# Pads in front of each bucket, a tile table laid over partitions, and row numbers kept aside in a routed two-layer graph and expert kernel

## What is computed

```python
x = x + gnn(layernorm(x), adj)      # two layers: scores h h^T, softmax, mask adj, three projections
x = x + ffn(layernorm(x))           # routed experts, below
# ffn, with 8 experts of width 64, on the 16384 tokens xt:
route_prob = softmax((xt @ enc_w + enc_b) @ sw_w + sw_b)
routes     = argmax(route_prob)                       # one expert e for each token
out        = (gelu(xt @ w1[e] + b1[e]) @ w2[e] + b2[e]) * max(route_prob)
```

## Time and profile before

| | |
|---|---|
| time, median of 3 executions (lowest, highest) | 2221.36 us (2217.87, 2224.03) |
| profiled execution | 2229.13 us |
| its span, first to last instruction | 2227.4 us |
| mean granted TensorE clock, share of full speed | 0.986 |
| PE, DVE, ACT, POOL busy, share of the span | 95%, 75%, 67%, 63% |
| graph stage | from 0 to about 1938 us of the span |
| hand-over, last count to first tile's normalise | 1938 to 1956 us |
| expert stage | 1956 to 2227 us |

### The profile page before, as it was taken

How to read it: one execution, slowest core, us unless ns; L and a number is a source line. 1 busy time by engine, 2 the same in 40 slices (tenths; PEclk the granted TensorE clock), 3 DMA queues, 4 the chain that set the end, 5 groups by cost and what they waited for, 6 DMA issues and landing times. The chain is left out here.

```text
span 2227.4 us, 56587 instructions
## 1 busy us (share of the span) xinstructions
PE 2116.7 (95%) x13576; PEld 2035.7 (91%) x13577; DVE 1661.4 (75%) x5442; ACT 1496.4 (67%) x3901; POOL 1405.0 (63%) x3274
## 2 busy tenths in 40 slices
PE   6999999999999999999999999999999999578886
PEld 5999999999999999999999998999999999456665
DVE  4777777777777777777777776777777777657775
ACT  4777777677676776677777766776777766356664
POOL 2556666666666666666666666666666666535555
PEclk9999999999999999999999999999999999789998
DMA  7101111111111111111111111111111111256664
GB/s 188 31 26 49 49 37 49 49 45 49 41 45 49 49 45 50 42 49 49 49 43 47 49 49 42 45 49 49 46 48 41 45 49 33 105 184 208 221 224 144
DMA packets 94261, 153.77 MB, mean 69 GB/s; under 512 B 17627, under 2 KB 70700, under 8 KB 93954
## 3 DMA queue, kind: packets, MB, share of 16 engines
q1 hardware_dynamic: 75844, 99.61, 15.1%
q0 software_dynamic: 17408, 50.62, 6.0%
q10 hardware_dynamic: 704, 0.10, 0.0%
HBM read 96.11 MB, written 57.32 MB: 69 GB/s over the span
## 5 line engine op out<-in xcount | busy, mean ns | idle before, releaser
L421 PE MATMUL bank<-wT_hi,hT_hi 128*128 128x384 f32 x2304 | 797.9, 346 | 11.4 <-issue 5.4
L423 PE MATMUL bank<-wT_hi,hT_lo 128*128 128x384 f32 x2304 | 774.5, 336 | 0.0
L422 PE MATMUL bank<-wT_lo,hT_hi 128*128 128x384 f32 x2304 | 773.0, 336 | 0.0
L421 PEld LDWEIGHTS bank<-wT_hi,hT_hi 128*128 128x128 f32 x2304 | 434.9, 189 | 19.2 <-ACT bank L614 11.1
L422 PEld LDWEIGHTS bank<-wT_lo,hT_hi 128*128 128x128 f32 x2304 | 435.0, 189 | 0.0
L423 PEld LDWEIGHTS bank<-wT_hi,hT_lo 128*128 128x128 f32 x2304 | 433.8, 188 | 0.0
L1145 POOL TENSOR_TENSOR hT_lo<-hT,hT_hi 128x384 fp32r<-128x384 f32 x256 | 263.5, 1029 | 23.9 <-ACT hT_hi L679 22.4
L674 ACT ACTIVATE hT<-bank 128x384 f32<-128x384 f32 x256 | 126.1, 493 | 202.5 <-PE bank L413 180.9
L650 ACT CAST right_hi<-bank 128x384 fp32r<-128x384 f32 x256 | 123.0, 480 | 180.1 <-PE bank L423 179.2
L1548 POOL DMA_INDIRECT out_dram<-out_rows,tok x144 | 144.1, 1000 | 136.4 <-DVE out_rows L1519 100.7
L1200 POOL TENSOR_SCALAR_AFFINE_SELECT deltaT_hi<-turned_hi 128x128 fp32r<-128x128 f32 x256 | 87.7, 343 | 216.0 <-ACT turned_hi L656 208.5
(11 more groups left out here) (183 smaller groups left out, 5142.9 us busy)
## 6 DMA issues: line engine op xcount, KB each, us to landing
tok<-buckets SPq DMA_DIRECT2D x72, 388.0 KB
x_in<-in_x_dram SPq DMA_DIRECT2D x128, 192.0 KB, 2.5
x_res<-in_x_dram SPq DMA_DIRECT2D x128, 192.0 KB, 2.4
adj_in<-in_adj_dram SPq DMA_DIRECT2D x128, 64.0 KB, 2.4
buckets<-pads SPq DMA_DIRECT2D x9, 388.0 KB
out_dram<-out_rows,tok POOLq DMA_INDIRECT x144
buckets<-rows,dest_words POOLq DMA_INDIRECT x128, 2.8
w_top<-in_L_ffn_w_dram SPq DMA_DIRECT2D x2, 768.0 KB
```

The costliest lines, as they stand in the source:

```text
L421: pe.matmul(o, hi, w_hi, start=False, stop=False, skip_group_check=True)
L422: pe.matmul(o, hi, w_lo, start=False, stop=False, skip_group_check=True)
L423: last = pe.matmul(o, lo, w_hi, start=False, stop=(c == C - 1), skip_group_check=True)
```

## The change

1. **Pads in front.** A bucket's rows now begin FRONT = 256 rows behind its start, and the pads stand in those first 256 rows. Their nine stores need no computed row any more; SP issues them in the graph stage, behind the three loads of step 26 (PAD_STEP). An expert's last tile no longer runs on into pads behind the bucket: it begins 256 rows before the bucket's end, and so holds again some rows of the tile before it (or pads, for an expert with one tile).
2. **Tile table over partitions.** `tile_table` has tile number n on partition n, with operands of 72x8 or 72x64 and a few 72x1; its results lie in a column and are turned into rows by PE. A further result, `again`, gives for each row of each tile a large number where the row is one that the tile before has had, so that it is not written twice.
3. **Row numbers aside.** In step j+2 POOL adds the `ID` words of `tok[k]` and `again` into `row_ids[k]` (semaphore `ids_kept`), and the stores take their row numbers from there. SP's load of tile j waits for the combine of tile j-8 and for `ids_kept` in place of `stored`.

```diff
@@ graph stage, SP
                     def first_steps(i, key):
                         step(i, key)
+                        if isinstance(i, int) and i == PAD_STEP:
+                            sp.wait_ge(pads_made, 1)
+                            for row in [e * CAP for e in range(E)] + [TAIL]:
+                                sp.dma_start(buckets[row:row + TILE, :]..., pads[:]).then_inc(pads_stored, 16)
...
                     steps(sp, first_steps)
-                    sp.wait_ge(pads_made, 1)
-                    sp.dma_start(buckets[TAIL:TAIL + TILE, :]..., pads[:]).then_inc(pads_stored, 16)
-                    sp.wait_ge(ends_ready, 1)
-                    for e in range(E):
-                        row = sp.value_load(end_words[0:1, e:e + 1], min_val=e * CAP, max_val=e * CAP + TOKENS)
-                        sp.dma_start(buckets[bass.ds(row, TILE), :]..., pads[:]).then_inc(pads_stored, 16)
@@ PE, behind the last count
+                    pe.wait_ge(table_done, 2)
+                    pe.transpose(rows_of, per_tile["row"][0:TILES, :], ident[0:TILES, 0:TILES])
+                    pe.transpose(experts_of, per_tile["expert_at_most"][0:TILES, :], ident[0:TILES, 0:TILES]
+                                 ).then_inc(table_turned, 1)
+                    pe.wait_ge(table_done, 3)
+                    pe.matmul(twice_of, per_tile["twice_wide"][0:TILES, :], ident[0:TILES, 0:TILES], ...
+                              ).then_inc(table_turned, 1)
@@ DVE, tile_table: the dependent steps now, each one small operation
   held -> rough -> rounded -> tiles_of -> lower_tiles -> tiles_upto -> behind -> expert -> own_end -> end
        -> in_buckets -> row -> (PE turns) -> tile_row, tile_expert -> twice_wide -> (PE turns) -> again (x2)
@@ POOL, setup: iotas of 1x512, 1x576, 1x8, 1x64 give way to six, each of 128 partitions and at most 64 elements
@@ expert stage, SP load
                         if past(j, RING):
-                            sp.wait_ge(stored[k % OUT_RING], 16 * T // OUT_RING * (j - RING - k % OUT_RING) + 16 * T)
+                            sp.wait_ge(y_ready, T * (j - RING) + T)
+                            sp.nop(nofuse=True)
+                            sp.wait_ge(ids_kept, j - RING + 1)
@@ expert stage, POOL
+                    def keep_ids(j, k):
+                        pool.wait_ge(tok_loaded[k], 16 // RING * (j - k) + 16)
+                        if past(j, RING):
+                            pool.wait_ge(stored[k % OUT_RING], 16 * T // OUT_RING * (j - RING - k % OUT_RING) + 16 * T)
+                        pool.nop(nofuse=True)
+                        pool.tensor_tensor(row_ids[k][:], tok[k][:, :, ID].bitcast(I32),
+                                           again[:, j, :] ..., ALU.add).then_inc(ids_kept, 1)
+
                     def store(j, k):
+                        pool.wait_ge(ids_kept, j + 1)
                         for t in range(T):
...
-                                bass.IndirectOffsetOnAxis(ap=tok[k][:, t, ID:ID + 1].bitcast(U32), axis=0),
+                                bass.IndirectOffsetOnAxis(ap=row_ids[k][:, t:t + 1].bitcast(U32), axis=0),
...
                     def step(i, k):
+                        if there(i - 2):
+                            keep_ids(i - 2, (k - 2) % RING)
                         if there(i - DEPTH):
                             store(i - DEPTH, (k - DEPTH) % RING)
```

More of the change, by code:

```diff
@@ L157, in build @@
             w2_spare_bottom = ring_sb(2, "w2_spare_bottom", [P, D], F32R)
[L159 to L166, removed]
+            per_tile = {}
+            for name, shape in (("bases", [P, E]), ("held", [P, E]), ("rough", [P, E]), ("rounded", [P, E]),
+                                ("tiles_of", [P, E]), ("lower", [P, E, E]), ("lower_tiles", [P, E, E]),
+                                ("tiles_upto", [P, E]), ("behind", [P, E]), ("skipped", [P, E]), ("skip", [P, 1]),
+                                ("expert", [P, 1]), ("expert_at_most", [P, 1]), ("experts", [P, E + 1]),
+                                ("ends", [P, E + 1]), ("own_end", [P, E + 1]), ("end", [P, 1]), ("number", [P, 1]),
+                                ("straight", [P, 1]), ("twice", [P, 1]), ("twice_wide", [P, P]), ("position", [P, T]), ("in_expert", [P, 1]), ("in_buckets", [P, 1]), ("row", [P, 1])):
+                per_tile[name] = sb(f"per_tile_{name}", shape, F32, gnn_ctx)
             x_loaded = [sem(f"x_loaded{k}") for k in range(2)]
@@ L1005, in tile_table @@
[L1005 to L1012, removed]
@@ L1013, in tile_table @@
[L1013 to L1015 removed]
+                        dve.wait_ge(table, 8)
+                        dve.tensor_reduce(o["expert"], o["behind"], AX_X, ALU.add).then_inc(table, 1)
+                        dve.tensor_tensor_reduce(o["skipped"], o["behind"], o["tiles_of"], 1.0, 0.0, ALU.mult, ALU.add,
+                                                 o["skip"]).then_inc(table, 1)
@@ L1016, in tile_table @@
                         dve.wait_ge(table, 11)
-                        dve.scalar_tensor_tensor(o["row"][:], o["numbers"][:, :, 0], float(TILE), o["rows_before"][:],
+                        dve.tensor_reduce(o["end"], o["own_end"], AX_X, ALU.add).then_inc(table, 1)
+                        dve.wait_ge(table, 12)
+                        dve.scalar_tensor_tensor(o["in_buckets"], o["expert"], float(CAP), o["in_expert"],
                                                  ALU.mult, ALU.add).then_inc(table, 1)
-                        dve.wait_ge(table, 12)
@@ L1020, in tile_table @@
-                        dve.tensor_scalar(tile_row[:], o["row"][:], float(TAIL), None, ALU.min).then_inc(tiles_ready, 1)
+                        dve.wait_ge(table, 14)
+                        dve.tensor_scalar(o["row"], o["end"], -float(TILE), o["in_buckets"][:, 0:1], ALU.add, ALU.min
+                                          ).then_inc(table_done, 1)
+                        dve.wait_ge(table_done, 2)
+                        dve.tensor_tensor(o["twice"], o["in_buckets"], o["row"], ALU.subtract).then_inc(table, 1)
@@ L1022, in constants @@
+                        for t in range(T):
+                            dve.tensor_scalar(again[:, :, t], twice_of, per_tile["position"][:, t:t + 1], float(2 * TOKENS),
+                                              ALU.is_gt, ALU.mult).then_inc(tiles_ready, 1)
                     def constants():
```

94 lines of the change are left out of this document (60 added, 34 removed).

## The result

The changed kernel takes 2162.1 us (median of 4 runs, 2160.5 to 2163.8) against 2221.7 us for the kernel before, run beside it: a ratio of 0.973 (95% interval 0.972 to 0.9745), 59.6 us less. I had forecast 2180 with a range of 2166 to 2206: the direction was right, and the time lies under the range.

What follows compares the result with a forecast made beforehand. The prediction took a ring over the store's landing, 3.53 us a tile, to bound the expert stage. Loop -36.8, drain +1 and hand-over -5.7 gave -41.5 us, from a median of 2221.36 to 2180 us, range 2166 to 2206.

Steps and rivals of the forecast that it cites:

- stops of 10.5 us: Expert loop: ACT's unnamed waits and a lower clock, estimated at 10.5 us, would remain after the change.
- the price of `keep_ids` on POOL: Expert loop: the added POOL operation costs 0.25 us a tile, between 0.17 and 0.53.
- A ring over the store's landing: Expert loop: combine, store, landing, load and normalise must fit into three steps, 10.6 us, setting 3.53 us a tile.
- POOL's pace: Expert loop after the change: POOL's two stores and `keep_ids` need 2.83 us, so the pace is 2.85 us a tile.
- The base: Old expert loop: 63 steps between first and last normalise take 226.9 us, from which the loop's gain was counted.
- PE's floor: Expert loop: PE needs 2.66 us a tile, read from the first tiles, whose tokens are there in advance.
- my rival with 0.15: Expert loop: PE sets the pace, 2.66 to 2.75 us a tile, `keep_ids` hiding between stores; 2168 us, chance 0.15.
- The first eight tiles: Start of the expert loop: these tiles don't change, 0 us.
- Hand-over: Graph to expert stage: without pad stores the first load goes out near 1947.2, -5.7 us (-4.6 to -7.6).
- Pads in the graph stage: Step 26 of the graph stage: nine pad stores fit into 13.5 us on SP and cost nothing, at worst some 5 us.
- The constants: Setup: the shorter iotas are off the path, 0 us.
- The drain: Behind the last normalise: POOL's stores are already back to back, and the few `keep_ids` there cost +1 us.

Runs made afterwards that it cites:

- before_fourth: The kernel before, unchanged, profiled in another execution with increments on time: 2220.5 us.
- wait_stored: The changed kernel with the load of tile j waiting again for the store of tile j-8 to land: 2216.1 us, ratio 0.997.
- ids_only: The kernel before with part 3 of the change alone (row numbers copied aside, load waits for the combine): 2171.1 us, ratio 0.977.
- after: The changed kernel itself, as first profiled: an execution of 2160.5 us, median 2162.1 us.
- ids_by_dve_c: The changed kernel with row numbers put together by DVE instead of POOL, all PE work kept, third run: 2161.3 us, ratio 0.973.
- less_pe_by_dve: The changed kernel without the third matmul of the experts' first layer, row numbers put together by DVE instead of POOL: 2156.9 us, ratio 0.971.
- table_longer: The changed kernel with ten dependent small DVE operations ahead of the tile table: 2164.4 us, ratio 0.973.
- after_again: The changed kernel, unchanged, run again in a group with late increments: 2222.7 us, ratio 0.997.
- after_third: The changed kernel, unchanged, once more on another chip, again with late increments: 2218.2 us, ratio 0.9965.

## Why the prediction was right, and where it was wrong

The time fell under the range because two terms of the sum were too high: stops of 10.5 us that the kernel doesn't have, and the price of `keep_ids` on POOL.

- **What bounds the kernel: right.** A ring over the store's landing at 3.53 us a tile; `before_fourth`, `wait_stored` and `ids_only` each show it. That the load is late, not slow, held too.
- **The stops: wrong, 10.5 us where nothing was.** Of the 226.9 us I let 10.5 stay as stops that "have nothing to do with the ring". After has none: its 63 steps are 63 x 2.68. They came from the execution that I had read, which had late increments (221.3 us in the clean one). Waits that no view could name were the sign of that, and I carried them over as if the kernel owned them.
- **POOL's pace: wrong, 2.85 for 2.68, another 10.7 us.** The price of `keep_ids` on POOL was mis-sized, 0.25 us for 0.08 by the rows (0.22 + 0.16 - 0.30), under the lower bound of 0.17 that I had given; I had taken the gap before a scatter (0.20) and a longer operation. POOL's 2.69 then no longer stands clear of PE's 2.68, and PE's floor holds, which rows 5 had right within 0.02. `ids_by_dve_c` beside `less_pe_by_dve` shows that PE it is. This was my rival with 0.15; it still gave 2168, because it kept the stops.
- **The base: 5.6 us.** The old loop was 221.3, not 226.9, which hides part of the two errors: -36.8 - 10.5 - 10.7 + 5.6 = -52.4, measured -52.5.
- **The first eight tiles: wrong, 0 for -2.7.** The ninth normalise already waits for a reloaded buffer, so the ring's first turn (5.17 us for that step in `before_fourth`, 2.65 in after) is in that stretch.
- **Hand-over: -4.6 for -5.7, at the small end of its range (-4.6 to -7.6).** I had the block end with DVE's table, near 1944.4. It does not: `table_longer` adds 2.1 us to the table, and the block ends no later for it. My price of the table was too high anyway (5.0 us for 6.0: 1934.54 to the end of `again`), and the 3.2 us from the end of POOL's last scatter to the next block were not in the sum. The agreement is in part luck: the block ended 8.7 us behind the last count where I had 6.4, and the first load went out 1.2 us behind that where I had 2.8.
- **Pads in the graph stage: right, 0.**
- **The constants: 0 for perhaps -1.1.** I called the iotas off the path. On POOL's timeline the two wide ones (0.59 and 0.95 us for 512 and 576 elements on one partition) stand ahead of the next `ln_t`: from the end of `hT_lo` to it 3.96 or 3.97 us with the old constants in all five traces and 2.86 to 2.88 in all fifteen with the new. The last count comes at 1937.2 + 0.6 in the mean of the five and 1935.7 + 0.6 in that of the fifteen, with 2 us of scatter either way. That fits 1.1 us less, but that the 1.1 us reach the last count is not shown, and the rest of the -2.3 lies within that scatter.
- **The drain: +2.1 for +1.** It isn't the price of `keep_ids`: `wait_stored` has them too and takes 21.0 us. POOL has the larger backlog: behind the last normalise after still issues 15 stores, the last one's end 7.6 us behind the last combine's; in `before_fourth` it is 12 stores and 5.8 us.
- **DMA: right that it does not bind.** Its share is 0.91 where I had put 0.8, as the pace is shorter, and `tok` is still on time (1.3 us of waits).
- **The range**, 2166 to 2206, was too narrow below because its low end took PE's pace together with the stops; without them it would have reached 2156.

## What to carry to other kernels

Before a trace is used for a sum, see whether its unnamed waits ("issue", "remote") belong to the kernel: compare two executions, and look whether landings are recorded in full. When a ring is opened, take the pace of the next engine from a stretch where nothing is late, and add nothing for what the old trace lost elsewhere. Small work beside DMA issues on POOL is cheap as long as POOL isn't the bound; where it is, count the meetings with DVE too. And a busy share near 100% doesn't name the bound: relieve each suspect alone, and then both.

## What the runs showed of the hardware that I had not expected

- In two of the five groups, increments of semaphores came 1 to 3 us late by the record once indirect stores and plain loads ran together (211 GB/s in `after_again`, 217 in `after_third`); the same kernel took 2162 us without them and 2218 to 2223 with them.
- An indirect DMA's issue on POOL took 1.12 us in place of 1.00 when it began with some 0.26 us of a DVE operation from SBUF to SBUF still to run, and 0.98 to 1.00 when 0.13 us or less were left. By the sum above that is why less work for PE made the kernel 7.3 us slower.
- Beside a `keep_ids` of 0.42 us DVE's `gelu_top` took 0.66 us in place of 0.30.
- DVE's first operation of the next block came 3.2 us behind the end of POOL's last scatter in after (1940.05 to 1943.24) and 2.9 in `table_longer` (1944.09 to 1947.04), though DVE's table ended 0.5 us before that scatter in the one and 1.5 us behind it in the other.
